# Late turns of a two-layer block: the output's affine step and gate on one engine, a late copy, other banks for the last down product

## The chip, the cores and the metric

The kernel runs on one core of one Trainium2 chip. The metric is the device time of one execution in microseconds (us); lower is better. The core has five engines that run their own instruction streams and meet at semaphores: TensorE (PE in the profile; PEld is its loading of weights), VectorE (DVE), ScalarE (ACT), GpSimd (POOL) and SyncE (SP), which issues the DMAs here. PSUM has eight banks of 512 fp32 numbers for each of 128 partitions; TensorE writes only there.

## The reference

Two residual layers over x of 8 x 256 tokens with 256 channels. The change touches the second alone:

```
xn = layernorm(x)
xc = silu(conv4(xn));  q, k = l2norm per head (xn Wq, xn Wk);  v = ln(xn Wv)
a  = sigmoid(xc Wgamma);  b = sigmoid(xc Wig) * k * v
mem = scan(a, b)                       # along the tokens
o = ln(ln(mem) * q) * gn_g + gn_b      # per head of 16; the last two are the affine step
o = o * sigmoid(xc Wog)                # the gate
x = x + o Wo + ffn(xn)                 # ffn: (sigmoid(xn W1) * (xn W2)) W3, ternary weights
```

The product with Wo is made from a high and a low part of o: ScalarE writes the high part (o_hi), VectorE the rest (o_lo).

## The kernel before

The first layer fills about 610 us and isn't touched. The second, `layer1` from line 933, treats the 2048 tokens in four groups of 512 (`GROUPS`), each of two sequences of 256, called half 0 and half 1 (`b` in the code). The work on a group is spread over two turns, and a turn holds three groups at different stages: `late` (scan, both norms, affine step, gate, output product, residual), `early` (projections, convolution's end, hidden layer, gates) and `ahead` (normalised and turned for the next turn). `turns` (line 1135) lists five turns: (none, 0, 1), (0, 1, 2), (1, 2, 3), (2, 3, none), (3, none, none). I call them turn 1 to turn 5. Each engine has its own function `turn` with the order of its work written out by hand, and an engine never passes a waiting instruction of its own.

Names that matter, with lines. On VectorE: `normalise` 1418 (four passes that write xn), `mlp_added` 1472 (adds the down product to X), `output_summed` 1513 and `output_normed` 1519 (the norm ahead of the affine step; a chain of small linked operations, and then two scalings, L1534, one for each half), `gated` 1190 (scale, shift, gate: three linked tensor operations of 128x512, L1144), `xn_low` 1149, `hidden` 1465, `convolve` 1428 (tap 0 is L1438, taps 1 to 3 are L1441), `output_low` 1536, `residual` 1541 and `scan` 1478, which opens the next turn. Before the change half 0 lies in SBUF (`o`) and its `gated` is on GpSimd, half 1 lies in bank 5 and its `gated` is on VectorE. On GpSimd also: `hidden_low` 1157, `through_input_gate` 1174 (frees `b_turn`) and `xn_low` of half 1 of the group ahead. On ScalarE: `queries_kept` 1311 (copies the queries for the next turn, and must wait for `ro_done` of the late group's `output_normed`), `decays` 1304, `xn_high` 1249, `gate` 1320, `hidden_high` 1287, `output_high` 1342. On TensorE: `xn_turn` 1621 and `o_turn` 1721 (transposes), `output` 1729 (twelve matmuls for a half), `b_turn` 1703, `ffn_up` 1649, `center_rows` 1713, `ffn_down` 1666. `ffn_up(0)` waits for `xn_low` of both halves.

TensorE's order at a turn's end is gate(2), gate(3), o_turn(0), o_turn(1), xn_turn(ahead, 1), output(0), output(1), and the next turn opens with b_turn(0), b_turn(1), ffn_up(0), center_rows(0), center_rows(1). The down product of the late group goes to banks 4 and 5, so it has to wait until the scaled memory has left them (`op_done0`, `mn_done`).

Of the kernel before, what the change touches and what calls it, by code (L numbers as in the profile page):

```python
# [5 lines left out]
ALU = mybir.AluOpType  # L6
# [10 lines left out]
D = 256  # L17
# [4 lines left out]
GROUPS = 4  # L22
GT = TOK // GROUPS
TPG = GT // P
BPG = BATCH // GROUPS
# [907 lines left out]
def layer1(nc, dram, keep, out):  # L933

    X, ident = keep["X"], keep["ident"]
    with ExitStack() as ctx:
# [173 lines left out]
        def pair(b):  # L1110
            return slice(2 * b, 2 * b + 2)
# [8 lines left out]
        def turned(ap):  # L1120
            return ap.rearrange("p (k n) -> p k n", k=KC)
# [68 lines left out]
        def gated(engine, late, b):  # L1190
            wait = waiter(engine, late)
            wait("on_done", b + 1)
            y = turned(banks[5][:]) if b else o[:, pair(b), :]
            inc(linked(engine, wait, f"o_link{b}", [
                (y, y, gn_g2, ALU.mult),
                (y, y, gn_b2, ALU.add),
                (o[:, pair(b), :], y, gates[:, 1 + late % 2, pair(b), :], ALU.mult)]), f"o_done{b}")

        @block.sync
        def _(sp):  # L1200
            for g in range(GROUPS):
                for b in range(BPG):
                    sp.wait_ge(S["res_done"], START + g * PER["res_done"] + b + 1)
                    inc(sp.dma_start(out[GT * g + SEQ * b:GT * g + SEQ * b + SEQ, :].rearrange("(a p) d -> p a d", p=P), X[:, TPG * g + 2 * b:TPG * g + 2 * b + 2, :]), f"stored{b}", 16)
            for n in range(2):
                sp.wait_ge(S[f"stored{n}"], START + 16 * GROUPS)

        @block.gpsimd
        def _(pool):
            pool.memset(xpad[:, :, :, 0:PAD], 0.0).then_inc(pad_zeroed, 1)  # L1210

            def turn(late, early, ahead):
                def convolved():
                    wait = waiter(pool, early)
                    for k in range(KC):
                        wait("conv_sig", k + 1)
                        inc(pool.tensor_tensor(cs[:, k, :], cv[:, k, :], cs[:, k, :], ALU.mult), "xc_done")
                    for k in range(KC):
                        wait("xc_hi_done", k + 1)
                        inc(pool.tensor_tensor(xc_lo[:, k, :], cs[:, k, :], xc_hi[:, k, :].bitcast(F32), ALU.subtract), "xc_lo_done")  # L1220

                if late is None:
                    xn_low(pool, early, 1)
                if late is not None:
                    memory_scaled(pool, late, 1)
                if early is not None:
                    hidden_low(pool, early, 1)
                    convolved()
                    hidden_low(pool, early, 2)
                    values(pool, early, 0)  # L1230
                    hidden_low(pool, early, 3)
                    hidden_low(pool, early, 4)
                if late is not None:
                    gated(pool, late, 0)
                if early is not None:
                    through_input_gate(pool, early, 0)
                    hidden_low(pool, early, 5)
                    through_input_gate(pool, early, 1)
                if ahead is not None:
                    xn_low(pool, ahead, 1)  # L1240

            turns(turn)

        @block.scalar
        def _(act):
            act.wait_ge(pad_zeroed, 1)

            def turn(late, early, ahead):
                def xn_high(g, b):
                    wait = waiter(act, g)  # L1250
                    wait("xn_turned", b + 1)
                    if b == 0:
                        wait("v_done", 0)
                        wait("up_done", 0)
                        wait("conv_step", 0)
                        wait("xn_lo_done0", 0)
                        wait("xn_lo_done1", 0)
                    src = turned(banks[b][:])
                    inc(act.activation(xn_hi[:, :, SEQ * b:SEQ * b + SEQ], src, ACT.Copy), "xn_hi_done")
                    inc(act.activation(xpad[:, :, b, PAD:PAD + SEQ], src, ACT.Copy), "xpad_done")  # L1260
# [80 lines left out]

                def output_high(b):
                    wait = waiter(act, late)
                    wait("o_turned", b + 1)
                    inc(act.activation(o_hi[:, b, :, :], turned(banks[4 + b][:]), ACT.Copy), "o_hi_done")

                if late is None:
# [27 lines left out]
                if early is not None:  # L1375
                    gate(0)
                    gate(1)
                    hidden(5)
                    queries_kept()
                    decays(1)  # L1380
                if ahead is not None:
                    xn_high(ahead, 0)
                if early is not None:
                    gate(2)
                    hidden_high(5)
                    gate(3)
                if late is not None:
                    output_high(0)
                    output_high(1)
                if ahead is not None:  # L1390
                    xn_high(ahead, 1)

            turns(turn)

        @block.vector
        def _(dve):
            def turn(late, early, ahead):
                links = [0, 0]

                def link(ins, g, which):  # L1400
# [71 lines left out]
                def mlp_added(b):  # L1472
                    wait = waiter(dve, late)
                    wait("down_done", b + 1)
                    x = X[:, late * TPG + 2 * b:late * TPG + 2 * b + 2, :]
                    inc(dve.tensor_tensor(x, x, turned(banks[4 + b][:]), ALU.add), "mlp_done")

                def scan(b):
                    wait = waiter(dve, late)
# [39 lines left out]
                def output_normed():  # L1519
# [10 lines left out]
                    inc(dve.tensor_tensor(s2[:], s2[:], rq[:], ALU.mult), "ro_done")  # L1530
                    wait("ro_done", 1)
                    for b in range(BPG):
                        y = turned(banks[5][:]) if b else o[:, pair(b), :]
                        inc(dve.tensor_tensor(heads(y), heads(o[:, pair(b), :]), each(s2[:, b, :]), ALU.mult), "on_done")  # L1534

                def output_low(b):
                    wait = waiter(dve, late)
                    wait("o_hi_done", b + 1)
                    inc(dve.tensor_tensor(o_lo[:, b, :, :], turned(banks[4 + b][:]), o_hi[:, b, :, :].bitcast(F32), ALU.subtract), "o_lo_done")

                def residual(b):
                    wait = waiter(dve, late)
                    wait("y_done", b + 1)
                    x = X[:, late * TPG + 2 * b:late * TPG + 2 * b + 2, :]
                    inc(dve.tensor_tensor(x, turned(banks[4 + b][:]), x, ALU.add), "res_done")

# [29 lines left out]
                    output_centered(1)  # L1576
                if early is not None:
                    hidden(4)
                if late is not None:
                    mlp_added(0)  # L1580
                    mlp_added(1)
                    output_summed()
                if ahead is not None:
                    normalise(ahead)
                if late is not None:
                    output_normed()
                    gated(dve, late, 1)
                if early is not None:
                    hidden(5)
                if ahead is not None:  # L1590
                    xn_low(dve, ahead, 0)
                if late is not None:
                    output_low(0)
                    output_low(1)
                if ahead is not None:
                    convolve(ahead, range(0, 2))
                if late is not None:
                    residual(0)
                    residual(1)

            turns(turn)

# [1 line left out]
        def _(pe):  # L1604
# [13 lines left out]
                return [lambda k, x=x: x[:, k, a:b] for x in (w_hi, w_lo)]  # L1618

            def turn(late, early, ahead):  # L1620
                def xn_turn(g, b):
                    wait = waiter(pe, g)
                    wait("xn_ready", 2 * b + 2)
# [42 lines left out]
                def ffn_down(b):  # L1666
                    wait = waiter(pe, late)
                    if b == 0:
                        for c in range(FFN_CHUNKS):
                            wait(f"h_lo_done{c}", 1)  # L1670
                        wait("hid_done", FFN_CHUNKS)
                        wait("op_done0", 1)
                    wait("mn_done", b + 1)
                    for t in range(2 * b, 2 * b + 2):
                        dst = banks[4 + b][:, D * (t % 2):D * (t % 2) + D]
                        for n, h in enumerate((h_hi, h_lo)):
                            for c in range(FFN_CHUNKS):
                                mm = pe.matmul(dst, h[:, place(late, c), P * t:P * t + P], w3[:, c, :], start=(n == 0 and c == 0), stop=(n == 1 and c == FFN_CHUNKS - 1))  # L1678
# [49 lines left out]

                def output(b):
                    wait = waiter(pe, late)  # L1730
                    wait("o_lo_done", b + 1)
                    for t in range(2):
                        mm = product(banks[4 + b][:, D * t:D * t + D], [lambda k, x=x: x[:, b, k, P * t:P * t + P] for x in (o_hi, o_lo)],
                                     [lambda k, x=x: x[:, k, :] for x in (wo_hi, wo_lo)])
# [35 lines left out]
                if early is not None:  # L1770
                    gate(2)
                    gate(3)
                if late is not None:
                    o_turn(0)
                    o_turn(1)
                if ahead is not None:
                    xn_turn(ahead, 1)
                if late is not None:
                    output(0)
                    output(1)  # L1780

            turns(turn)

# [92 lines left out]
```

## Time and profile before

| | |
|---|---|
| median of 3 runs | 878.27 us (878.25 to 881.27) |
| the profiled execution's own time | 880.21 us, of which the span of its profile is 878.3 us |
| busy in the span | PE 748.4 us (85%), DVE 650.7 us (74%), ACT 453.3 us (52%), POOL 412.3 us (47%) |
| second layer's turns start at (DVE's first of the turn) | 627.98, 678.98, 732.18, 785.38, 837.29 us |

A row of the timeline tells when an instruction started, how long it took, its engine, its line, what it writes and reads, and in brackets how long its engine had been idle in front of it and which instruction ended that wait. A line of a helper stands for all that call it: L1144 is every linked operation of `gated`, `values` and `memory_scaled`, L1610 every product. The names `rows` are the tiles vn, mem and o, `shared` the convolution and the decay, `lbank` any bank.

### The profile page before, as it was taken

What the parts mean: (1) busy time and instruction counts of PE and PEld (TensorE: products, weight loads), DVE (VectorE), ACT (ScalarE), POOL (GpSimd) and SP (SyncE); (2) the same over time, 40 slices, a digit from 0 to 9 for tenths busy, and PEclk for the clock granted to TensorE, in tenths of its full rate; (3) what the DMA queues carried; (4) which work ended last, traced back from release to release, by engine and by line L of the source; (5) the groups of instructions that cost most, each with busy time, mean ns of one, the idle gap of its engine ahead of it and who ended that gap; (6) DMA issues with size and microseconds to landing.
All of it is one profiled execution on the core that took longest, in us unless ns stands there. A gap on an engine that the chain in (4) does not pass through costs nothing. (4 is left out here: it accounts for less than half of the span.)

```text
span 878.3 us, 15217 instructions
## 1 busy us (share of the span) xinstructions
PE 748.4 (85%) x5602; PEld 644.3 (73%) x5602; DVE 650.7 (74%) x1146; ACT 453.3 (52%) x717; POOL 412.3 (47%) x335
## 2 busy tenths in 40 slices
PE   3278799999999999999999999996278979969763
PEld 2266688888888878888888888885156858768652
DVE  6999867787777777776687686653555999989765
ACT  4246646665655645655655665563554544435310
POOL 2344543354366467575345244334336473745611
PEclk9579999999999999999999999999589999989876
DMA  5011121201001111011000000001200000000000
GB/s 153 25 38 40 36 83 35 57 26 44 20 15 50 28 36 38 23 47 32 3 20 20 2 21 20 3 2 62 97 1 1 1 0 25 1 25 1 0 25 24
DMA packets 21389, 25.89 MB, mean 29 GB/s; under 512 B 4419, under 2 KB 17091, under 8 KB 21061
## 3 DMA queue, kind: packets, MB, share of 16 engines
q1 hardware_dynamic: 21316, 24.93, 9.7%
q8 instruction: 45, 0.74, 0.4%
q14 instruction: 28, 0.22, 0.1%
HBM read 14.83 MB, written 3.28 MB: 21 GB/s over the span
## 5 line engine op out<-in xcount | busy, mean ns | idle before, releaser
L594 DVE TENSOR_REDUCE neg_max<-s_pair 128x4 f32<-128x1024 f32 x127 | 155.0, 1221 | 79.3 <-PE s_pair L806 79.1
L447 ACT ACTIVATE probs<-t_pair 128x1024 f32<-128x1024 f32 x128 | 131.3, 1026 | 140.3 <-PE t_pair L831 140.0
L346 POOL TENSOR_TENSOR hid<-g,hid 128x512 f32<-128x512 f32 x64 | 82.3, 1285 | 181.8 <-DVE g L705 147.6
L340 POOL TENSOR_TENSOR hid_lo<-hid,hid_hi 128x512 fp32r<-128x512 f32 x64 | 85.9, 1342 | 99.0 <-ACT hid_hi L457 98.8
L806 PE MATMUL s_pair<-K,Q 96*128 96x256 f32 x508 | 84.7, 290 | 15.6 <-DVE neg_max L594 9.3
L806 PEld LDWEIGHTS s_pair<-K,Q 96*128 96x128 f32 x508 | 75.8, 194 | 24.4 <-issue 8.1
L831 PE MATMUL t_pair<-Q,K 104*128 104x512 f32 x256 | 85.9, 418 | 0.3 <-DMA Q<-max_parts 0.3
L873 PE MATMUL down<-w_hi,hid_hi 128*128 128x256 f32 x256 | 83.9, 328 | 0.7 <-POOL hid_lo L340 0.7
L1144 POOL TENSOR_TENSOR rows<-rows,par 128x512 f32<-128x512 f32 x24 | 33.7, 1404 | 84.0 <-DVE rows L1503 55.3
L846 PE MATMUL misc<-probs,V 128*32 128x256 f32 x1024 | 69.8, 391 | 3.4 <-DVE kc L564 2.5
L873 PE MATMUL down<-w_lo,hid_hi 128*128 128x256 f32 x256 | 72.1, 282 | 0.0
L873 PE MATMUL down<-w_hi,hid_lo 128*128 128x256 f32 x256 | 72.1, 282 | 0.0
L873 PEld LDWEIGHTS down<-w_hi,hid_hi 128*128 128x128 f32 x256 | 48.2, 188 | 26.7 <-issue 24.6
L734 PE MATMUL gate<-xn_hi,w_hi 128*128 128x256 f32 x256 | 57.0, 304 | 0.0
L697 DVE SCALAR_TENSOR_TENSOR g<-g,gate 128x512 f32<-128x512 f32 x64 | 42.8, 669 | 18.8 <-ACT g L460 18.7
L468 ACT ACTIVATE g<-g 128x512 f32<-128x512 f32 x64 | 40.2, 628 | 29.4 <-DVE g L697 29.4
L734 PE MATMUL up<-xn_hi,w_hi 128*128 128x256 f32 x256 | 52.5, 287 | 0.0
L734 PE MATMUL up<-xn_lo,w_hi 128*128 128x256 f32 x256 | 52.3, 286 | 0.0
L734 PE MATMUL up<-xn_hi,w_lo 128*128 128x256 f32 x256 | 52.3, 287 | 0.0
L734 PE MATMUL gate<-xn_hi,w_lo 128*128 128x256 f32 x256 | 51.4, 282 | 0.0
L734 PE MATMUL gate<-xn_lo,w_hi 128*128 128x256 f32 x256 | 51.3, 282 | 0.0
L734 PEld LDWEIGHTS gate<-xn_hi,w_hi 128*128 128x128 f32 x256 | 43.9, 192 | 6.8
(251 smaller groups left out, 1978.9 us busy)
## 6 DMA issues: line engine op xcount, KB each, us to landing
stage<-in_ternary SPq DMA_DIRECT2D x18, 256.0 KB, 2.9
Q<-q_hi SPq DMA_DIRECT2D x64, 64.0 KB, 2.0
stage<-in_scales SPq DMA_DIRECT2D x8, 384.0 KB, 3.4
X<-in_x SPq DMA_DIRECT2D x8, 256.0 KB, 3.8
Q<-q_lo SPq DMA_DIRECT2D x32, 64.0 KB, 2.0
Q<-max_parts SPq DMA_DIRECT2D x128, 4.0 KB
out<-X SPq DMA_DIRECT2D x8, 256.0 KB, 2.2
shared<-in_l1w SPq DMA_DIRECT2D x1, 1536.0 KB, 6.5
```

The source lines that it names most:

```text
L340: pool.tensor_tensor(hid_lo[:, m % 2, :, :].rearrange("p a n -> p (a n)"), hid[:, m % 2, :], hid_hi[:, m % 2, :, :].rearrange("p a n -> p ...
L346: pool.tensor_tensor(hid[:, m % 2, :], g[:, m % 2, :], hid[:, m % 2, :], ALU.mult).then_inc(S["hid_done"], 1)
L447: act.activation(probs[:, u % 2, th, :], t_pair[:], ACT.Exp, scale=SCALE).then_inc(S["probs_done"], 1)
L468: act.activation(g[:, m % 2, :], g[:, m % 2, :], ACT.Tanh, scale=GELU_B).then_inc(S["t_done"], 1)
L594: dve.tensor_reduce(neg_max[:, u % 2, 4 * jp:4 * jp + 4], score_banks(u, jp)[:].rearrange("p (s n) -> p s n", n=SEQ), AX_X, ALU.max, negat ...
L697: dve.scalar_tensor_tensor(out=g[:, m % 2, :], in0=g[:, m % 2, :], scalar=1.0, in1=gate[:], op0=ALU.add, op1=ALU.mult).then_inc(S["u_done" ...
L734: mm = pe.matmul(out, lhs[a][k], rhs[b][k], start=(n == 0), stop=(n == 3 * KC - 1))
L806: mm = pe.matmul(score_banks(u, jp)[:, 512 * j + SEQ * s:512 * j + SEQ * s + SEQ], Q[0:KROWS, quad, 2 * jp + j, P * s:P * s + P], K[0:KROW ...
L831: mm = pe.matmul(t_pair[:, 512 * jp:512 * jp + 512].rearrange("p (j n) -> p j n", j=2), K[rows, quad, hq, P * th:P * th + P], Q[rows, quad ...
L846: mm = pe.matmul(misc[32 * j:32 * j + 32, 0:SEQ], V[:, th, h, :], probs[:, u % 2, th, SEQ * j:SEQ * j + SEQ], start=(th == 0), stop=(th == ...
L873: mm = pe.matmul(down[:, D * t:D * t + D], h[:, m % 2, n, P * t:P * t + P], w[:, a, n, 2 * D:3 * D], start=(a == 0 and t == 0 and n == 0 a ...
L1144: ins = engine.tensor_tensor(*step)
```

## The change

- `gated` of both halves is on VectorE, and both halves lie in banks 4 and 5 (the second scaling of `output_normed` writes there). GpSimd loses `gated(0)`; its `through_input_gate(0)` comes directly behind `hidden_low(4)`.
- VectorE does `xn_low(ahead, 0)` ahead of both `gated`, `hidden(5)` behind them, tap 0 of the convolution ahead of `output_low` and tap 1 behind it.
- ScalarE does `queries_kept` and `hidden_high(5)` behind gate(2), gate(3) and xn_high(ahead, 1), just ahead of `output_high`. This holds for turn 1 too, which has no late group.
- TensorE does xn_turn(ahead, 1) ahead of both `o_turn`.
- In turn 5 the down product goes to banks 6 and 7 and doesn't wait for the scaled memory; VectorE adds it behind `output_summed`; and half 1 goes ahead of half 0 from `gated` to the store (`halves`).

```diff
@@ gated @@
-            y = turned(banks[5][:]) if b else o[:, pair(b), :]
+            y = turned(banks[4 + b][:])
@@ sync @@
+                halves = (0, 1) if g < GROUPS - 1 else (1, 0)
+                for n, b in enumerate(halves):
+                    sp.wait_ge(S["res_done"], START + g * PER["res_done"] + n + 1)
@@ gpsimd @@
                     hidden_low(pool, early, 4)
-                if late is not None:
-                    gated(pool, late, 0)
+                    through_input_gate(pool, early, 0)
                 if early is not None:
-                    through_input_gate(pool, early, 0)
                     hidden_low(pool, early, 5)
@@ scalar @@
                     hidden(5)
-                    queries_kept()
                     decays(1)
                 if ahead is not None:
                     xn_high(ahead, 0)
                 if early is not None:
                     gate(2)
-                    hidden_high(5)
                     gate(3)
-                if late is not None:
-                    output_high(0)
-                    output_high(1)
                 if ahead is not None:
                     xn_high(ahead, 1)
+                if early is not None:
+                    queries_kept()
+                    hidden_high(5)
+                if late is not None:
+                    for b in halves:
+                        output_high(b)
@@ vector, mlp_added @@
-                    inc(dve.tensor_tensor(x, x, turned(banks[4 + b][:]), ALU.add), "mlp_done")
+                    inc(dve.tensor_tensor(x, x, turned(banks[(4 if early is not None else 6) + b][:]), ALU.add), "mlp_done")
@@ vector, output_normed @@
-                        y = turned(banks[5][:]) if b else o[:, pair(b), :]
+                        y = turned(banks[4 + b][:])
@@ vector, order @@
-                if late is not None:
-                    mlp_added(0)
-                    mlp_added(1)
+                    if late is not None:
+                        mlp_added(0)
+                        mlp_added(1)
+                if late is not None:
                     output_summed()
+                    if early is None:
+                        mlp_added(0)
+                        mlp_added(1)
                 if ahead is not None:
                     normalise(ahead)
                 if late is not None:
                     output_normed()
-                    gated(dve, late, 1)
+                if ahead is not None:
+                    xn_low(dve, ahead, 0)
+                if late is not None:
+                    for b in halves:
+                        gated(dve, late, b)
                 if early is not None:
                     hidden(5)
                 if ahead is not None:
-                    xn_low(dve, ahead, 0)
-                if late is not None:
-                    output_low(0)
-                    output_low(1)
+                    convolve(ahead, range(0, 1))
+                if late is not None:
+                    for b in halves:
+                        output_low(b)
                 if ahead is not None:
-                    convolve(ahead, range(0, 2))
-                if late is not None:
-                    residual(0)
-                    residual(1)
+                    convolve(ahead, range(1, 2))
+                if late is not None:
+                    for b in halves:
+                        residual(b)
@@ tensor, ffn_down @@
-                        wait("op_done0", 1)
-                    wait("mn_done", b + 1)
+                    if early is not None:
+                        if b == 0:
+                            wait("op_done0", 1)
+                        wait("mn_done", b + 1)
-                        dst = banks[4 + b][:, D * (t % 2):D * (t % 2) + D]
+                        dst = banks[(4 if early is not None else 6) + b][:, D * (t % 2):D * (t % 2) + D]
@@ tensor, order @@
-                if late is not None:
-                    o_turn(0)
-                    o_turn(1)
                 if ahead is not None:
                     xn_turn(ahead, 1)
                 if late is not None:
-                    output(0)
-                    output(1)
+                    for b in halves:
+                        o_turn(b)
+                    for b in halves:
+                        output(b)
```

The waits of `output_high`, `output_low`, `residual` and `output` count in the order of `halves`.

## Rows read from the trace of the kernel before

**Rows 1.** Stretches of turns 3 and 5: PE, PEld, DVE, ACT, POOL busy, PEclk, DMA share

```profile
732.20:785.40 53.20, 45.49 (x249) 38.49 (x250) 49.16 (x93) 24.60 (x44) 29.98 (x22) 0.94 0.03 11
837.30:878.30 41.00, 17.86 (x100) 16.50 (x100) 25.08 (x54) 3.65 (x6) 7.99 (x6) 0.70 0.06 20
```

**Rows 2.** Chain that ended last, turn 5: start us, us, engine, what, line

```profile
848.70 8.08 PE lbank L1678 x48
...
857.41 1.28 DVE s L1517 x2
...
863.11 1.66 POOL rows L1144
...
867.50 1.13 PE lbank L1726 x4
...
870.03 4.90 PE lbank L1610 x24
874.96 0.69 DVE X L1545
```

**Rows 3.** Timeline of ScalarE, turn 5: the last square ahead of the sums

```profile
852.33 0.63 ACT L1340 ACTIVATE osq<-rows 128x512 f32<-128x512 f32 x1 [0.69 <-DVE rows L1510]
```

**Rows 4.** Durations of L1144 on VectorE by shape: count, ns min/median/max, first and last start

```profile
L1144 DVE TENSOR_TENSOR lbank<-lbank,par x24: 690/699/700, 659.4 to 864.4; 128x512 f32<-128x512 f32 x24
```

**Rows 5.** Timeline of VectorE, end of turn 2 and start of turn 3

```profile
713.00 1.71 DVE L1426 TENSOR_SCALAR osq<-X,l_mv,l_rstd 128x256 f32<-128x256 f32 x4
...
719.58 1.43 DVE L1144 TENSOR_TENSOR lbank<-lbank,par 128x512 f32<-128x512 f32 x2
...
727.39 2.05 DVE L1438 TENSOR_SCALAR shared<-xpad,conv 128x512 f32<-128x512 f32 x2 [0.65 <-ACT xpad L1260]
...
732.18 2.42 DVE L1484 TENSOR_TENSOR_SCAN rows<-shared,lbank 128x256 f32<-128x256 f32 x4 [0.21 <-PE lbank L1710]
```

**Rows 6.** Timeline of GpSimd, end of turn 2

```profile
711.03 2.56 POOL L1161 TENSOR_TENSOR h_lo<-l_hid,h_hi 128x512 fp32r<-128x512 f32 x2
719.01 3.00 POOL L1144 TENSOR_TENSOR rows<-rows,par 128x512 f32<-128x512 f32 x2 [5.42 <-DVE rows L1534]
```

**Rows 7.** Timeline of TensorE, end of turn 2: the turned output

```profile
723.42 1.97 PE L1726 MATMUL lbank<-ident,rows 128*128 128x128 f32 x8 [5.40 <-POOL rows L1144]
```

**Rows 8.** Durations of normalise's passes, xn_low and tap 0 on VectorE, columns as in rows 4

```profile
L1426 DVE TENSOR_SCALAR osq<-X,l_mv,l_rstd x16: 399/403/1393, 628.0 to 767.5; 128x256 f32<-128x256 f32 x16
...
L1155 DVE TENSOR_TENSOR l_xn_lo<-xpad,l_xn_hi x4: 692/1174/1659, 631.1 to 775.5; 128x512 fp32r<-128x512 f32 x4
...
L1438 DVE TENSOR_SCALAR shared<-xpad,conv x8: 533/1078/1594, 632.1 to 782.1; 128x512 f32<-128x512 f32 x8
```

**Rows 9.** Timeline of ScalarE, end of turn 1: the queries' copy, the last xn_high

```profile
669.46 1.05 ACT L1317 ACTIVATE q_kept<-qk 128x1024 f32<-128x1024 f32 x1
...
675.02 0.60 ACT L1260 ACTIVATE xpad<-lbank 128x512 f32<-128x512 f32 x1
```

**Rows 10.** Timeline of GpSimd, end of turn 1: hidden_low(5) and xn_low(ahead, 1)

```profile
673.62 1.28 POOL L1161 TENSOR_TENSOR h_lo<-l_hid,h_hi 128x512 fp32r<-128x512 f32 x1 [2.74 <-ACT h_hi L1292]
...
676.07 1.38 POOL L1155 TENSOR_TENSOR l_xn_lo<-xpad,l_xn_hi 128x512 fp32r<-128x512 f32 x1
```

**Rows 11.** Timeline of TensorE, start of turn 2: b_turn(0), first of ffn_up(0)

```profile
674.28 0.60 PE L1710 MATMUL lbank<-ident,rows 128*128 128x128 f32 x4
...
677.71 0.70 PE L1662 MATMUL lbank<-l_xn_hi,tern 128*128 128x512 f32 x2 [0.87 <-POOL l_xn_lo L1155]
```

**Rows 12.** Stretches, columns as in rows 1: TensorE's gap, then the output of turn 4

```profile
718.00:723.40 5.40, 0.02 (x1) 0.00 (x0) 5.26 (x8) 4.27 (x8) 4.23 (x4) 0.73 0.01 2
...
828.60:836.30 7.70, 7.08 (x32) 6.68 (x32) 2.08 (x3) 1.32 (x3) 3.74 (x4) 0.50 0.07 23
```

**Rows 13.** Timeline of ScalarE, turn 3: the sigmoid of hidden chunk 2

```profile
747.30 0.60 ACT L1285 ACTIVATE sig<-lbank 128x512 f32<-128x512 f32 x1 [0.74 <-PE lbank L1662]
```

**Rows 14.** Timeline of VectorE, turn 3: hidden(2), which reads it

```profile
747.95 0.68 DVE L1470 TENSOR_TENSOR l_hid<-sig,lbank 128x512 f32<-128x512 f32 x1
```

More of the change, by code:

```diff
@@ L1201, in _ @@
             for g in range(GROUPS):
-                for b in range(BPG):
-                    sp.wait_ge(S["res_done"], START + g * PER["res_done"] + b + 1)
+                halves = (0, 1) if g < GROUPS - 1 else (1, 0)
+                for n, b in enumerate(halves):
+                    sp.wait_ge(S["res_done"], START + g * PER["res_done"] + n + 1)
                     inc(sp.dma_start(out[GT * g + SEQ * b:GT * g + SEQ * b + SEQ, :].rearrange("(a p) d -> p a d", p=P), X[:, TPG * g + 2 * b:TPG * g + 2 * b + 2, :]), f"stored{b}", 16)
@@ L1248, in turn @@
             def turn(late, early, ahead):
+                halves = (0, 1) if early is not None else (1, 0)
                 def xn_high(g, b):
@@ L1343, in output_high @@
                     wait = waiter(act, late)
-                    wait("o_turned", b + 1)
+                    wait("o_turned", halves.index(b) + 1)
                     inc(act.activation(o_hi[:, b, :, :], turned(banks[4 + b][:]), ACT.Copy), "o_hi_done")
@@ L1397, in turn @@
             def turn(late, early, ahead):
+                halves = (0, 1) if early is not None else (1, 0)
                 links = [0, 0]
@@ L1537, in output_low @@
                     wait = waiter(dve, late)
-                    wait("o_hi_done", b + 1)
+                    wait("o_hi_done", halves.index(b) + 1)
                     inc(dve.tensor_tensor(o_lo[:, b, :, :], turned(banks[4 + b][:]), o_hi[:, b, :, :].bitcast(F32), ALU.subtract), "o_lo_done")
@@ L1542, in residual @@
                     wait = waiter(dve, late)
-                    wait("y_done", b + 1)
+                    wait("y_done", halves.index(b) + 1)
                     x = X[:, late * TPG + 2 * b:late * TPG + 2 * b + 2, :]
@@ L1620, in turn @@
             def turn(late, early, ahead):
+                halves = (0, 1) if early is not None else (1, 0)
                 def xn_turn(g, b):
@@ L1730, in output @@
                     wait = waiter(pe, late)
-                    wait("o_lo_done", b + 1)
+                    wait("o_lo_done", halves.index(b) + 1)
                     for t in range(2):
```

## The prediction

> **What bounds it now.** I read the stretches turn by turn first. In turn 3, as in its twin turn 2, VectorE is busy 49.16 of 53.20 us, TensorE 45.49 [rows 1]: VectorE sets the pace, and its unfilled time is mostly the end of the turn. In turn 5 nothing overlaps: VectorE 25.08 and TensorE 17.86 us of 41.00, a pure chain [rows 1]. The chain that ended last shows it: down product 848.70 to 856.8, sums from 857.41, GpSimd's affine step from 863.11, transposes at 867.50, output product 870.03 to 874.93, last residual [rows 2]. The timelines of all engines at the ends of turns 1 and 2 came last, to see what stands behind each wait.
>
> **Turn 5, down product in other banks.** The squares that the sums need are ready at 852.33 + 0.63 = 852.96 [rows 3], but the sums start at 857.41 [rows 2], because the two adds that wait for the down product stand ahead. Freed, the product (8.08 us here, of which the first part at the lower clock) starts when the centring ends at about 841 and is over by 850, well under the norm. So the second sum starts at 853.02 and the two adds behind it take 1.2 us as anywhere; the norm's chain starts at 854.83, where it now starts at 857.41 + 1.28 = 858.7. Gain 3.9 us. Late next is the norm's chain itself, which no edit shortens.
>
> **Turn 5, affine step and gate.** GpSimd takes 3.00 us for scale and shift [rows 6] and 1.3 for the gate: 863.11 to 867.46, then transposes at 867.50. VectorE needs 0.70 for each operation [rows 4], and 2.08 for the linked three of a half: in turn 2 they start at 719.58 [rows 5] and the next instruction at 721.66. Both halves: 4.2 us. By times shifted by -3.9: half 1 starts at 859.8, is gated at 861.95, turned and copied by ScalarE by 863.75; half 0 is gated at 864.0, turned from 864.07, and TensorE is free for the output at 865.05. From 865.05 to the last residual at 4.90 + 0.03 us, up to 0.6 more if the clock never rises [rows 2]: residual at 870.0 to 870.5 against 874.96. I take 870.15 for its start: the turn gains 4.8 in all (4.4 to 5.7; the upper end has the clock rising three microseconds into the product).
>
> **Ends of turns 2 and 3.** Added on VectorE: 2.08 us. What goes is VectorE's wait of 2.1 us in three pieces for ScalarE's copies, which stand behind GpSimd's affine step and the transposes [rows 6, 7]. And some VectorE operations are held up beside a GpSimd one: a pass of normalise takes 0.40 alone and up to 1.39, xn_low 0.69 and up to 1.66, an operation of tap 0 0.53 and up to 1.59, each longest one where GpSimd ran beside it [rows 8]; tap 0's pair here took 2.05 for 1.06 [rows 5]. The change moves these meetings. GpSimd's through_input_gate(0) now follows hidden_low(4) at 713.59 [rows 6], in the middle of normalise, which starts at 713.00 [rows 5]: +1.0, as in turn 1 (bounds 0 and 1.3, one whole GpSimd operation). xn_low and tap 0 fall into GpSimd's idle time: -1.0 each. The pieces, on the clock of turn 2: both scalings done at 720.55, xn_low 720.5, gated(0) 721.1 to 723.2, gated(1) to 725.3, hidden(5) to 725.9, tap 0 to 726.8. ScalarE stands at hidden_high(5) until 726.0 though half 0 is already turned; then it copies half 0 to 727.15; output_low(0) ends at 727.9 and output(0) starts, where it now starts at 725.94. Its twelve matmuls and the next twelve take 5.12 at the lower clock, so the second residual runs at about 732.9 and the scan starts at 733.5, against 732.18 [rows 5]: +1.3. Bounds: +1.5 with all at the lower clock, +0.5 if it rises early in output(1).
>
> The clock: in the gap of 5.40 us TensorE's granted clock fell to the lower level, 1.2 GHz (mean 0.73), and in turn 4's output it stayed there for 7.7 us (0.50) [rows 12]. In the new order TensorE has xn_turn(1) until 719.7, then two transposes of 1 us each at 723.3 and 725.4, and nothing until 727.9 (the eight transposes take 1.97 [rows 7]). That is as empty, so I price outputs at the lower level.
>
> TensorE is the second pace-setter: the sigmoid for hidden(2) ends at 747.90 and hidden(2) starts at 747.95 [rows 13, 14], a slack of 0.05; turns 2 and 4 show the same. So what counts is TensorE's own delay. Now ffn_up(0) starts 0.3 behind the scan's start; in the new order b_turn(1) must wait for the second residual at 733.5, and ffn_up(0) starts at about 734.25, where it now starts at 732.5: +1.75. I take **+1.7 for each of the two turn ends**, 3.4 in all (2.0 to 4.6 over both, the upper end with the clock still low in ffn_up).
>
> Tap 1, which reads two SBUF tensors, would newly run beside GpSimd's through_input_gate(1) and xn_low. No row shows that; its nearest, xn_low on VectorE, gives 0 to 1.0 for each of its two operations. Both fit under the wait for output(1), so I count nothing; they would cost if the outputs were fast. The Trainium skill (SBUF — State Buffer, "two separate sides") says that VectorE with two SBUF inputs and a GpSimd operation hold a shared pair of ports exclusively and the loser waits for the whole instruction. By it tap 1 would end near 731.1 and no turn could shorten even with fast outputs; the row of xn_low agrees with it.
>
> **End of turn 4.** There is no ahead group. gated(0) starts at 824.7, gated(1) ends at 828.9, hidden(5) at 829.55, its high part at 830.2, and half 0's copy at 830.75; output(0) starts at 831.5 against 831.19. +0.3, less what an earlier rise gives: **+0.1** (-0.5 to +0.4).
>
> **End of turn 1.** This is the edit with the worst price. queries_kept takes 1.05 and 0.24 us [rows 9]. Where it stands now it hides under gates that TensorE delivers later. hidden_high(5), which now runs between the gates at 672.92 and starts GpSimd's tail at 673.62 [rows 10], goes behind xn_high(1), which ends at 675.6 [rows 9], and behind queries_kept: it ends at 677.2. On GpSimd hidden_low(5), through_input_gate(1) and xn_low(1) queue in order behind it, 1.24 apart: 677.26, 678.5, 679.75, ending at 680.95, where xn_low now starts at 676.07 [rows 10]. b_turn(1) moves to 679.85 and ffn_up(0) from 677.71 [rows 11] to 681.0: +3.3. Of this, 0.47 and 0.48 us of waits in front of center_rows and ffn_up(1) are absorbed: +2.35 at the full clock. But TensorE is then idle from 674.9 to 679.85, 4.95 us. In the gap of rows 12 the clock was down for 2.9 of 5.4 us, so I count it as down: ffn_up(0)'s eight matmuls take 3.4 for 1.9 us and center_rows' sixteen up to 3.4 for 1.7. The penalty is 0.9 to 2.7. On TensorE: +3.3 to +5.0. I take **+4.1**. hidden(2) has no slack here either, so VectorE inherits it.
>
> **Sum.** +4.1 + 3.4 + 0.1 - 4.8 = +2.8 us. The profiled execution's span of 878.3 goes to 881.1 and its own time of 880.21 to 883.0. The median of the runs shown is 878.27; the difference of 1.9 is what lies around the span in a profiled execution. I add 2.8 to the median: 881.1 us. A measurement of this kernel can tell about 0.5%, 4.4 us, from no change: 873.9 to 882.7.
>
> **Rivals.**
> 1. *The turns even out, the last one pays* (faster). TensorE's clock stays at the upper level, 2.4 GHz, at each boundary, normalise slips in between two GpSimd operations, and tap 1 isn't held up. Turn 1 costs 2.35; an end of turn 2 or 3: scalings done 1.0 earlier, output(0) at 726.9, 2.8 us for both outputs, scan at 730.6, -1.6 each; turn 4 -0.3; turn 5 -5.7. Sum -6.9, 871.4 us. For it: the gaps are broken by transposes. Against: the gap of rows 12 ended with the clock down, and the new ones hold as little work. A half-way case, where the ends of turns 2 and 3 cost nothing, gives 4.1 + 0.1 - 4.8 = -0.6: 877.7.
> 2. *TensorE turns into the bound at each boundary* (slower). One mechanism: the output product starts 2 us later from the lower clock, and as in turn 4 that holds 7.7 us [rows 12], which reaches through b_turn into ffn_up(0) of the next turn. Place: first products of turns 2, 3, 4. Price: 5.0 at turn 1, 2.6 at each of turns 2 and 3 (0.9 more than forecast), 0.4 at turn 4, and -4.4. Sum +6.2, 884.5 us. It decides from the point where the clock is still low 0.7 us into ffn_up.
> 3. *Only turn 5 moves.* If hidden_high(5) weren't late in turn 1 (were TensorE's start of turn 2 not bound by xn_low) and the ends cost nothing: -4.7, 873.6. The wait on xn_low is plain in rows 11, so this has little.
>
> **Chances.** Forecast (879 to 882.7) 0.46; half-way case (874 to 879) 0.17; rival 1 with what lies near it 0.08; rival 3 0.03; rival 2 (above 882.7) 0.26. So faster by over 0.5% is 0.11, within 0.5% 0.63, slower 0.26. The range leaves out most of rivals 1 and 3 and the far end of rival 2: 875.3 to 885.0.
>
> **What would show it.** Right: ffn_up(0) of turn 2 starts 3 us or more later than at 677.71, with PEclk at 0.5 in front of it; turns 2 and 3 each longer than 53.2 us by 1 to 2.6 from one ffn_up(0) to the next; in turn 5 the sums directly behind the squares and the time from the first scaling to the end shorter by about 0.9. Wrong: turn 2 starts on time; normalise keeps its 1.7 us; output(0) of turns 2 and 3 starts before 727 on the old clock; the clock is up throughout.

## The result and the profile after

The changed kernel takes 879.7 us (median of 20 runs, 878.02 to 883.13), the kernel before, over as many, 877.08 (875.22 to 881.27): ratio 1.003, interval 1.0019 to 1.0042, so 2.6 us more: little, but the interval leaves out 1. The forecast was 2.8 us more, on a median of three runs that lay 1.2 us above that of twenty. Two executions among the experiments below, e2's profiled one (1568 us) and one of e4's (1824 us), took about twice as long as all others and count in no ratio, so e2 has no landmarks and stands here again as e7.

The profiled executions alone would mislead: the span after is 877.7 us, below the 878.3 before. The first layer, which the change doesn't touch, ended 2.5 us earlier in that execution (the second layer starts at 625.46 against 627.98), and over the profiles below it ends anywhere from 623.7 to 628.0. So I compare the second layer by its own landmarks on VectorE. Each number is worked out from starts in the timeline: from the layer's first normalise to hidden(2) of turn 2, from there to hidden(2) of turns 3 and 4, on to the scan of turn 5, and from that to the last residual.

| us | to hidden(2), turn 2 | to turn 3's | to turn 4's | to turn 5's scan | turn 5 | sum |
|---|---|---|---|---|---|---|
| before | 66.75 | 53.22 | 53.20 | 36.14 | 37.67 | 246.98 |
| after | 70.48 | 55.03 | 54.83 | 35.80 | 32.86 | 249.00 |
| difference | +3.73 | +1.81 | +1.63 | -0.34 | -4.81 | +2.02 |
| forecast | +4.1 | +1.7 | +1.7 | +0.1 | -4.8 | +2.8 |

The first column also holds the first part of turn 1, which the change doesn't touch and which differs between executions: the turn's second normalise starts 37.11 us after the layer's start in the kernel before and 36.57 in the changed one. Counted from that normalise on, hidden(2) of turn 2 comes after 33.91 us, for 29.64 (+4.27), and the sum of the differences is +2.56, as much as the runs' 2.6.

Timelines of the changed kernel: the start of turn 2 on GpSimd and TensorE, against rows 10 and 11.

```profile
674.25 1.80 POOL L1161 TENSOR_TENSOR h_lo<-l_hid,h_hi 128x512 fp32r<-128x512 f32 x1 [6.45 <-ACT h_hi L1292]
676.01 1.26 POOL L1178 TENSOR_TENSOR rows<-qk,gates 128x512 f32<-128x512 f32 x1
677.23 1.18 POOL L1155 TENSOR_TENSOR l_xn_lo<-xpad,l_xn_hi 128x512 fp32r<-128x512 f32 x1
```

```profile
677.32 1.11 PE L1723 MATMUL lbank<-ident,rows 128*128 128x128 f32 x4 [5.49 <-POOL rows L1178]
678.67 1.19 PE L1673 MATMUL lbank<-l_xn_hi,tern 128*128 128x512 f32 x2 [0.23 <-POOL l_xn_lo L1155]
```

ffn_up(0) starts 53.21 us after the layer's start, where it started 49.73 after it [rows 11]: 3.5 later, and 4.0 later counted from the second normalise. Behind the gap of 5.49 us it runs at the lower clock, as this stretch shows (the columns are those of rows 1):

```profile
678.60:682.20 3.60, 3.53 (x8) 2.81 (x9) 3.60 (x6) 0.00 (x0) 0.00 (x0) 0.50 0.00 0
```

VectorE at the end of turn 2, against rows 5:

```profile
714.23 2.70 DVE L1428 TENSOR_SCALAR osq<-X,l_mv,l_rstd 128x256 f32<-128x256 f32 x4
...
721.67 0.68 DVE L1155 TENSOR_TENSOR l_xn_lo<-xpad,l_xn_hi 128x512 fp32r<-128x512 f32 x1
...
727.00 0.99 DVE L1440 TENSOR_SCALAR shared<-xpad,conv 128x512 f32<-128x512 f32 x2
728.26 1.29 DVE L1541 TENSOR_TENSOR o_lo<-lbank,o_hi 128x512 fp32r<-128x512 f32 x2 [0.27 <-ACT o_hi L1345]
729.47 3.05 DVE L1443 SCALAR_TENSOR_TENSOR shared<-xpad,conv,shared 128x512 f32<-128x512 f32 x2
732.44 0.68 DVE L1547 TENSOR_TENSOR X<-lbank,X 128x512 f32<-128x512 f32 x1
734.47 0.69 DVE L1547 TENSOR_TENSOR X<-lbank,X 128x512 f32<-128x512 f32 x1 [1.36 <-PE lbank L1620]
```

xn_low and tap 1 in the same place of the kernel before:

```profile
722.25 1.66 DVE L1155 TENSOR_TENSOR l_xn_lo<-xpad,l_xn_hi 128x512 fp32r<-128x512 f32 x1
...
729.37 1.40 DVE L1441 SCALAR_TENSOR_TENSOR shared<-xpad,conv,shared 128x512 f32<-128x512 f32 x2
```

The operations that are held up beside GpSimd have changed places: normalise takes 2.70 us for 1.71, xn_low 0.68 for 1.66, tap 0 0.99 for 2.05, tap 1 3.05 for 1.40. And the last residual waits 1.36 us for the output product, which ran at the lower clock:

```profile
729.00:734.00 5.00, 4.99 (x23) 4.99 (x24) 4.11 (x4) 0.00 (x0) 2.96 (x3) 0.50 0.00 0
```

VectorE in turn 5, against rows 2:

```profile
856.50 1.46 DVE L1519 TENSOR_REDUCE s<-osq 128x32 f32<-128x512 f32 x2
857.88 1.27 DVE L1478 TENSOR_TENSOR X<-X,lbank 128x512 f32<-128x512 f32 x2
859.07 0.23 DVE L1528 TENSOR_TENSOR lbank<-s,rq 128x64 f32<-128x64 f32 x1
...
862.69 1.30 DVE L1536 TENSOR_TENSOR lbank<-rows,s 128x512 f32<-128x512 f32 x2
864.03 1.43 DVE L1144 TENSOR_TENSOR lbank<-lbank,par 128x512 f32<-128x512 f32 x2
...
874.46 0.69 DVE L1547 TENSOR_TENSOR X<-lbank,X 128x512 f32<-128x512 f32 x1 [1.75 <-PE lbank L1620]
```

The sums stand directly behind the centring, the adds behind them without a wait. From the scan at 841.60 the norm starts 17.5 us later, where it started 21.4 later (858.7 from 837.29).

### The profile page after: what moved, and what is told of

The parts are those of the page before. It is cut to its first block and busy times, and to the rows that moved or that the text cites. A ratio compares the mean times of both kernels' runs of the same rounds, so it can differ in the third digit from the quotient of the medians.

```text
span 877.7 us, 15219 instructions
## 1 busy us (share of the span) xinstructions
PE 750.4 (85%) x5602; PEld 646.9 (74%) x5602; DVE 657.8 (75%) x1158; ACT 453.4 (52%) x717; POOL 395.5 (45%) x323
## 5 line engine op out<-in xcount | busy, mean ns | idle before, releaser
L1161 POOL TENSOR_TENSOR h_lo<-l_hid,h_hi 128x512 fp32r<-128x512 f32 x20 | 27.7, 1392 | 54.7 <-ACT h_hi L1292 54.7
```

## The experiments

All ratios are against runs of the kernel before on the same chip. The landmarks of all runs but e2, as above:

| us | to hidden(2), turn 2 | to turn 3's | to turn 4's | to turn 5's scan | turn 5 | sum |
|---|---|---|---|---|---|---|
| e1: turn 1's hidden_high(5) back | 66.40 | 55.08 | 54.94 | 35.81 | 32.88 | 245.11 |
| e3: before + banks in turn 5 | 65.67 | 53.20 | 53.24 | 35.95 | 33.84 | 241.90 |
| e4: input gate later | 70.23 | 54.20 | 53.11 | 35.41 | 32.64 | 245.59 |
| e5: TensorE busy, start of turn 2 | 68.72 | 54.39 | 54.50 | 35.59 | 32.75 | 245.95 |
| e6: TensorE busy, ends of 2 to 4 | 70.07 | 53.81 | 53.75 | 34.20 | 31.51 | 243.34 |
| e7: before + all of turn 5 | 66.26 | 53.22 | 53.24 | 36.04 | 31.63 | 240.39 |
| e8: e7 + TensorE busy, turns 4, 5 | 65.90 | 53.24 | 53.21 | 39.87 | 30.50 | 242.72 |
| e9: e8 with an earlier start | 66.39 | 53.26 | 53.24 | 33.42 | 30.51 | 236.82 |
| e10: changed kernel, all mended | 66.35 | 52.95 | 52.91 | 34.04 | 30.50 | 236.75 |

How far a landmark moves where nothing was changed: with the old order of the ends, turn 3's column is 53.20 to 53.26 in all five kernels. With the new order it moves by up to 0.64 (54.39 in e5 for 55.03), by when the clock rises in the output product. The first column moves by up to 1.1 (66.75 before, 65.67 in e3), and all of that lies ahead of turn 1's second normalise. The last two columns move by over 1 where the clock of the output product differs.

**e1: turn 1 alone put back.**

```diff
                     gate(2)
+                    if late is None:
+                        hidden_high(5)
                     gate(3)
                 if ahead is not None:
                     xn_high(ahead, 1)
                 if early is not None:
                     queries_kept()
-                    hidden_high(5)
+                    if late is not None:
+                        hidden_high(5)
```

> The changed kernel with one edit taken back: in turn 1 alone hidden_high(5) stands between gate(2) and gate(3) again. My account (late GpSimd tail, then a cold TensorE at the start of turn 2): ffn_up(0) of turn 2 starts 3 us earlier after turn 1's first normalise, the granted clock is at its upper level there, and the kernel gets 3.3 to 4.5 us faster than the changed one, so about 1 to 2 us faster than the kernel before. Rival (the turn ends on VectorE are the whole loss, turn 1's delay is absorbed): under 1 us.

Measured: 876.46 us, ratio 1.0001 (0.9985 to 1.0016), against 1.003 for the changed kernel; hidden(2) of turn 2 comes 4.08 us sooner (3.78 counted from the second normalise), and each later column stays within 0.11. GpSimd's tail and ffn_up(0) are back to 0.5 us behind their old places, counted so:

```profile
669.27 1.27 POOL L1161 TENSOR_TENSOR h_lo<-l_hid,h_hi 128x512 fp32r<-128x512 f32 x1 [3.23 <-ACT h_hi L1292]
```

```profile
673.38 0.70 PE L1676 MATMUL lbank<-l_xn_hi,tern 128*128 128x512 f32 x2 [0.86 <-POOL l_xn_lo L1155]
```

One instruction of 0.6 us on ScalarE, moved behind the last gate and four copies, was the largest loss of the change. Three details of the expectation missed. By the ratios 2.5 us come back, where 3.3 to 4.5 were expected. The kernel equals the kernel before, where it was to be 1 to 2 us faster. And the clock wasn't up throughout: it fell inside ffn_up(0) (the later pairs took 1.05 us for 0.63).

**e5: delay and clock apart.** Matmuls that nobody reads keep TensorE busy while it waits for b_turn(1) of turn 2. `filler(n)` issues n of them, each 128x512, into bank 2.

```diff
                     b_turn(0)
+                    if late == 0:
+                        waiter(pe, late)("gates_done", TPG)
+                        filler(24)
                     b_turn(1)
```

> The changed kernel, with 24 matmuls that nobody reads (128x512, into bank 2, which is free there) between b_turn(0) and b_turn(1) of turn 2 alone, so that TensorE has work in the gap of 5.5 us. It parts the price of turn 1's end into delay and clock. My account: ffn_up(0) starts as late as in the changed kernel, but it and center_rows run at the upper clock; the gap from the layer's start to hidden(2) of turn 2 gets 1.7 us shorter (0.9 to 2.7), so 1.5 to 2 us off the whole. Rival (the 4.1 us is delay alone): no difference from the changed kernel.

Measured: hidden(2) at 68.72, 1.76 us sooner than in the changed kernel. The ratio is 1.0003 (0.9986 to 1.002), 2.4 us under the changed kernel; the intervals overlap. The stretch of ffn_up(0), with its granted clock:

```profile
678.00:681.80 3.80, 3.36 (x21) 3.04 (x22) 3.69 (x6) 0.93 (x2) 0.18 (x1) 1.00 0.00 0
```

Counted from turn 1's second normalise, hidden(2) of turn 2 comes after 29.64 us in the kernel before, 33.91 in the changed one and 31.97 here. So of the 4.27 us by which the end of turn 1 grew, 1.94 were the clock, and 2.33, the delay, stay.

**e4: GpSimd out of normalise's way.**

```diff
                     hidden_low(pool, early, 4)
-                    through_input_gate(pool, early, 0)
+                    if late is None:
+                        through_input_gate(pool, early, 0)
                 if early is not None:
                     hidden_low(pool, early, 5)
+                    if late is not None:
+                        through_input_gate(pool, early, 0)
```

> The changed kernel, with through_input_gate(0) on GpSimd behind hidden_low(5) in turns 2 to 4, out of normalise's way. My account: normalise's four passes take 1.7 us again where they took 2.7, and the scans of turns 3 and 4 come 0.8 to 1.0 us earlier each, 2 us in all against the changed kernel; GpSimd's tail gets 1.3 us longer and ends at about the second residual, still ahead of ffn_up(0). Rival (output's product is paced by ScalarE and TensorE, not by normalise): turn length unchanged within 0.3 us. A third outcome: ffn_up(0) now waits for xn_low(1) on GpSimd, and the gain is given back.

Measured: ratio 0.9991 (0.9974 to 1.0008), 3.4 us under the changed kernel, and 3.4 in the landmarks. normalise takes 1.71 and 1.69 us again. Turn 2's end came 0.83 us sooner, as expected; turn 3's 1.72, more than normalise can give, since the clock rose inside the output product there. The two ends, VectorE's second residual of each:

```profile
734.45 0.69 DVE L1550 TENSOR_TENSOR X<-lbank,X 128x512 f32<-128x512 f32 x1 [1.29 <-PE lbank L1623]
...
787.64 0.69 DVE L1550 TENSOR_TENSOR X<-lbank,X 128x512 f32<-128x512 f32 x1 [0.30 <-PE lbank L1623]
```

**e6: TensorE busy at the ends of turns 2 to 4**, with 16 such matmuls ahead of the transposes, 5 between them and 6 behind.

> The changed kernel, with matmuls that nobody reads in TensorE's gaps at the ends of turns 2 to 4: 16 ahead of the transposes, 5 between them, 6 ahead of the output product. My account: both outputs run at the upper clock in 2.9 us where they took 5.2; VectorE is then held by tap 1 beside GpSimd until 732.4 on the changed kernel's clock, so the scans of turns 3 and 4 come 1.2 to 1.5 us earlier each and that of turn 5 about 1 to 2 us, 4 us in all. Rival (the outputs are hidden under tap 1 anyway): under 1 us in all.

Measured: ratio 0.9967 (0.9951 to 0.9984), 5.5 us under the changed kernel. The ends of turns 2 and 3 are 1.2 and 1.1 us shorter, that of turn 4 1.6, 3.9 in all, as expected. Another 1.35 came in turn 5, which this edit doesn't touch: the clock rose there 2 us ahead of the last residual, in the changed kernel only at the product's last matmuls.

**e2, e3, e7: turn 5 by itself.** e3 is the kernel before with these edits and no others:

```diff
-                        wait("op_done0", 1)
-                    wait("mn_done", b + 1)
+                    if early is not None:
+                        if b == 0:
+                            wait("op_done0", 1)
+                        wait("mn_done", b + 1)
-                        dst = banks[4 + b]...
+                        dst = banks[(4 if early is not None else 6) + b]...
```

and mlp_added behind output_summed in turn 5. e2 and e7 are one kernel, which also gates both halves on VectorE there, half 1 first.

> The kernel before with the down product of turn 5 in banks 6 and 7 and its adds behind the sums, nothing else; GpSimd keeps gated(0). My account: turn 5 shorter by 3.9 us, ratio 0.9955; the affine step's share of turn 5 is what this lacks against the run with all of turn 5's edits, 0.9 us. Rival (the split of the affine step was the better one there): this is as fast as that run or faster.

> The kernel before with the edits of turn 5 alone: down product in banks 6 and 7, both halves gated on VectorE in banks, half 1 first. My account: turns 1 to 4 as before, turn 5 shorter by 4.8 us (4.4 to 5.7), so 872 to 873 us where the kernel before has 877, ratio 0.9945. Rival (the gain of turn 5 in the profile is the clock's luck): a ratio above 0.998.

> The kernel before with the edits of turn 5 alone, once more, for an undisturbed profile. Turn 5 from its first scan to the last residual: 32.9 us as in the changed kernel, against 37.7 before; turns 2 to 4 of 53.2, 53.2 and 52 us. Ratio 0.9945.

Measured: e3 0.9958 (0.9944 to 0.9973); e2 0.9938 (0.9917 to 0.9959); e7 0.9931 (0.991 to 0.9952). Turn 5 takes 33.84 us in e3, 3.8 less than before. With the affine step it takes 32.86 and 32.88 (changed kernel, e1), and 31.63 in e7, where 32.9 was expected. There the clock rose 2.3 us into the output product, and the two last residuals start 1.42 us apart, for 2.44 in the changed kernel.

```profile
864.12 0.69 DVE L1548 TENSOR_TENSOR X<-lbank,X 128x512 f32<-128x512 f32 x1 [1.03 <-PE lbank L1619]
865.54 0.69 DVE L1548 TENSOR_TENSOR X<-lbank,X 128x512 f32<-128x512 f32 x1 [0.73 <-PE lbank L1619]
```

**e8, e9: can the clock be had where it matters?** Both are e7 with unread matmuls at the end of turn 4 and in turn 5. In e8 those of turn 4 go to bank 2 and wait for the last gate; in e9 they go to bank 6 and wait for the last sigmoid:

```diff
                     if ahead is None and early is not None:
-                        waiter(pe, early)("gates_done", TPG)
-                        filler(20)
+                        waiter(pe, early)("sig_done", FFN_CHUNKS)
+                        filler(21)
```

> The same with unread matmuls in TensorE's gaps of turns 4 and 5 alone: 20 ahead of turn 4's transposes, and in turn 5 12 behind the sums, 9 behind the first scaling, 5 between the transposes. If the clock is what makes the last outputs slow, both of turn 4's take 2.9 us for 5.5 and turn 5's the same, so 2.3 us less at the end of turn 4 and 2.0 to 2.5 in turn 5: 4.5 us below the run with turn 5's edits alone, ratio 0.989. Rival (latencies between engines, not the rate of TensorE, set these ends): under 1.5 us. A third outcome: the unread matmuls delay the transposes and cost as much as they bring.

> The kernel before with turn 5's edits, and the unread matmuls of turns 4 and 5 as in the last such run but for turn 4's: 21 into bank 6, which is free once the last sigmoid has read it, so they wait for no gate and start 5 us earlier, while the clock is still up. My account (clock): the time from hidden(2) to the scan of turn 5 is 34.0 us against 36.0 in the run with turn 5's edits alone, and turn 5 takes 30.5 as in the last run: ratio 0.989 to 0.991. Rival (latency): 36 us stays. If the earlier loss came from crowding the transposes and not from the late start, the scan of turn 5 is late again.

Measured: e8 0.9961 (0.9944 to 0.9978), 2.1 us **slower** than e7 (the intervals overlap, the landmarks say 2.3), which was the third outcome named; and e9 0.9888 (0.9865 to 0.991), 866.92 us, the lowest median of all. e8 shows how such work backfires. From TensorE's timeline:

```profile
823.82 6.62 PE L1633 MATMUL lbank<-l_hi 128*128 128x512 f32 x20 [5.03 <-ACT gates L1332]
830.29 1.03 PE L1742 MATMUL lbank<-ident,rows 128*128 128x128 f32 x8
```

The gate they wait for stands behind hidden_high(5) on ScalarE, so they began after a gap of 5.03 us, at the lower clock, took 6.62 us (e9's 21 took 4.94), and pushed the transposes back: these start 34.1 us behind hidden(2), for 27.5 in e7 and 27.6 in e9. In e9 the unread matmuls start while the clock is up, and are over in time:

```profile
819.11 4.94 PE L1633 MATMUL lbank<-l_hi 128*128 128x512 f32 x21
```

```profile
826.50:829.60 3.10, 3.10 (x28) 3.10 (x27) 1.19 (x3) 0.00 (x0) 1.42 (x2) 1.00 0.02 5
```

Turn 5's scan comes 33.42 us behind hidden(2) for 36.04, and turn 5 takes 30.5 in both, for 31.63 in e7. In turn 5 the unread matmuls begin at the lower clock, behind a longer gap than in e8's turn 4. From e9's timeline:

```profile
846.48 5.06 PE L1633 MATMUL lbank<-l_hi 128*128 128x512 f32 x11 [7.15 <-DVE s L1520]
```

The clock is at the upper level from 852.2 to behind the output product, and the transposes start at 854.70, as soon as VectorE has gated their half. So the late start did harm where the unread matmuls outlasted the wait, and none where they were over in time.

**e10: do the terms add up?** The changed kernel with e1's and e4's edits and unread matmuls in turns 2 to 5.

> The changed kernel with each of its losses mended at once: turn 1's hidden_high(5) between the gates, through_input_gate(0) behind hidden_low(5) in turns 2 to 4, and unread matmuls in TensorE's gaps of turns 2 to 5. If the three terms add up as I account for them: hidden(2) of turn 2 comes 66 us after the layer's start (70.5 in the changed kernel), turns 2 and 3 last 52.8 us each (55.0, 54.8), turn 5's scan 34 us behind hidden(2), turn 5 30.5: 236 to 237 us for the layer, ratio 0.985 to 0.989. Rival (the losses share one cause, so that mending two brings no more than one): ratio above 0.993.

Measured: ratio 0.9904 (0.9881 to 0.9927), 868.1 us; landmarks 66.35, 52.95, 52.91, 34.04, 30.50, sum 236.75. In the landmarks they add up, as expected; the ratio is a little above the expected 0.985 to 0.989. Its turns 2 and 3 are 0.3 us shorter than those of the kernel before. Whether that is the new order of the ends isn't shown: no run puts unread matmuls into turns 2 and 3 of the old order. And e9, with the old order there, has the same sum (236.82). What holds it now is tap 1 beside GpSimd; from its VectorE timeline:

```profile
725.77 3.22 DVE L1449 SCALAR_TENSOR_TENSOR shared<-xpad,conv,shared 128x512 f32<-128x512 f32 x2
728.91 1.27 DVE L1553 TENSOR_TENSOR X<-lbank,X 128x512 f32<-128x512 f32 x2
```

No wait stands in front of the residuals any more, and tap 1 takes 1.8 us more than the 1.40 of the kernel before.

## Why the prediction was right, step by step

- **Turn 5, +0.0 off.** -4.81 for -4.8. e3 gives the down product 3.8 for the 3.9 worked out; the affine step is the rest, 1.0 for 0.9. That the sum fits to 0.01 is luck: the output product started 0.3 us sooner than worked out, and took as much longer to the last residual (5.39 us for 5.1), as the clock rose only at its end. In e7 the same edits gave 6.0, above the stated 4.4 to 5.7, by an earlier rise.
- **End of turn 1.** +3.73 for +4.1, or +4.27 without the untouched first part of the turn. The mechanism held: e1 takes back 3.78 of it. The split, 2.35 of delay and the rest (1.75) the clock, is what e5 measured: 2.33 and 1.94. But the 2.35 were 3.3 less 0.95, and both were too small, by 0.7 and 0.8, which cancels by luck. ffn_up(0) started 4.0 later, as hidden_low(5) took 1.80 us for 1.28 and b_turn(1) ran at the lower clock; and in e5, where it started 4.1 later, 1.7 were absorbed. The clock cost fell on ffn_up(0) alone, whose later pairs took 1.05 us for 0.63; center_rows, which the forecast let double as well, took 2.32 for 2.31.
- **Ends of turns 2 and 3.** +1.81 and +1.63 for +1.7 each. The parts: normalise +0.99 (for +1.0), xn_low and tap 0 -0.98 and -1.06 (for -1.0 each), the lower clock in the outputs, a last residual that waits for them. e4 and e6 take 0.8 and 1.2 off the end of turn 2 separately, so both pieces are on the path; e5, which has neither edit, takes 0.6 off by an earlier rise of the clock alone, which is a measure of their error. In e4 normalise itself is 0.99 shorter.
- **Tap 1 beside GpSimd**, for which no row of before existed, took 3.05 us for 1.40. It was taken at nothing in the sum, as hidden under the wait for the output: the wait of 1.36 us behind it shows that it was. The Trainium skill (SBUF — State Buffer, "two separate sides") has the loser of the shared pair of ports wait for a whole instruction, and by that the forecast had tap 1 end near 731.1 on the old clock. It ended at 732.52, where hidden(2) stands 1.21 us later than before (695.94 for 694.73), so at 731.3: the trace agrees. In e10 it is the bound.
- **End of turn 4.** -0.34 for +0.1. The start of output(0) was right; the clock rose at 840.0, during output(1), and the second residual came 1.92 us behind the first, where it had come 2.53 behind.
- **Rivals.** The first fell on its condition: the clock fell in TensorE's gaps at all four ends, and output(0) ran at the lower level in turns 2 to 4. The second didn't happen because the clock rose at 734.2 and 788.8, before ffn_up(0), not behind it. The third is what e1 looks at: without turn 1's loss the changed kernel equals the kernel before by its runs (1.0 us less by its landmarks from turn 1's second normalise on), and isn't 4.7 us faster, so the ends count.

What stays open: when in an execution the clock rises. It moved single columns of the tables by up to 1.4 us between kernels with the same code there. Of the 0.6 us between the landmarks' +2.0 and the runs' +2.6, 0.54 are the untouched first part of turn 1. In e1 and e10 the landmarks so counted and the runs differ by 1 us, and why stays open too.

## What to carry to other kernels

An edit that shortens the end of a pipeline is often written for all its turns; price each turn by itself, the first above all, where another engine's queue stands behind the moved instruction. Here the turn that drains gave 4.8 us, and the turns that were already full took more than that back. Moving VectorE's operations away from GpSimd's made new meetings here: 1.0 and 1.1 us were gained at the end of turn 2, and 1.0 and 1.65 lost. List all meetings in the new order before counting one as gained.

## What the runs showed of the hardware

- Unread matmuls in a gap paid where they were over when the wait was: 21 of them gave 2.6 us at the end of turn 4 (e9). 20 of them, behind a gap of 5.03 us and at the lower clock, outlasted it and cost 3.8 (e8). In turn 5 they began at the lower clock too, behind 7.15 us of idleness, but ended in time, and turn 5 took 30.50 us for 31.63 (e9, e7).
- Beside GpSimd the two operations of tap 1, which read two SBUF tensors, took 3.05 to 3.22 us for 1.40 (changed kernel, e10), and the four passes of normalise 2.70 for 1.71.
- Kernels that differ only in the second layer ended the first anywhere between 623.7 and 628.0 us. Differences of under 4 us between two spans say nothing here. Landmarks inside the changed part repeat to 0.06 us (turn 3's column in five kernels), or to 0.64 where the clock rises inside them.
